# Attention by key blocks: eight score matmuls in one stretch, then the values of four heads, with the row maxima 20 turns ahead

## The chip, the cores and the metric

The kernel runs on one core of a Trainium2 chip. Its engines are TensorE (PE; its weight loads are listed as PEld), VectorE (DVE), ScalarE (ACT), GpSimd (POOL) and SyncE (SP, which only issues DMAs here). The metric is device time in microseconds, the median of several runs.

## The reference, cut to what matters

Four layers follow each other on a tensor of 8 x 1024 x 256: a recurrent mixer, a feed-forward layer, a self-attention layer and the feed-forward layer again. Only the attention layer is touched by the change:

```python
qkv = (x @ Wqkv + bqkv).reshape(B, L, 3, 16, 16)          # B = 8, L = 1024, 16 heads of 16
q, k, v = qkv[:, :, 0], qkv[:, :, 1], qkv[:, :, 2]
scores = einsum('bqhd,bkhd->bhqk', q, k) / sqrt(16)
scores = scores + slopes[None, :, None, None] * -abs(pos[None, :] - pos[:, None])
probs = softmax(scores, axis=-1)
out = einsum('bhqk,bkhd->bqhd', probs, v).reshape(B, L, 256)
x = x + (out @ Wout + bout)                                # x was layer-normed before Wqkv
```

## The kernel before, in words

The attention layer (`attention`, from L1383) works on groups of four heads: 8 batches x 4 groups = 32 groups, numbered `g`. For a group it computes every score twice.

The first time is for the maxima. `find_maxima` on TensorE (L1639) multiplies one query block of 128 rows with half of the keys (512), for one head: a "turn", 64 turns for a group. The result fills one PSUM bank. VectorE reduces it to a maximum for each query (L1896). Below, r0, r1, r2, r3 are four turns in a row. The second time is for the values. `attend` on TensorE (L1701) computes scores with keys on the partitions: one key block of 128 keys against half of the queries (512), for one head, already shifted by the maximum, which travels as an extra row of the operand. ScalarE applies the exponential to two heads at a time (L1814), and `weigh` (L1655) multiplies the result with the values. Below, c0 to c3 are the four column score matmuls of a key block, one for each head, and V is its values.

Scores contract over 64 rows only, so a head takes half of the array: row group `rg` 0 or 1 (`tile_position=(first, 0)`). A matmul on row group 0 and one on row group 1 can run side by side. The values have 17 columns, so four heads take four column tiles (`tile_position=(0, i * SLOT)`) over all 128 rows. A pair is two heads, one on each row group. `use = 2 * t + pair` counts the pairs of scores; 16 key block steps `t` make a group (8 key blocks for each half of the queries), 512 steps in all. The bias needs a correction inside one 512 wide half: `add_block_bias` (L1560) adds two matmuls of 64 columns for each score matmul of a block that is `here`. Half of the turns and half of the key blocks are.

PSUM has eight banks. Banks 0 to 3 hold the column scores, two banks for each `use`, so that pair 0 and pair 1 alternate (`scores[use % 2]`). Bank 4 holds the values. Banks 5, 6 and 7 are a ring, `misc`: every turn of the maxima takes the next of the three, and so does every other product of the layer (queries and keys, values of the tokens, transposes, the output projection). Who takes a bank waits first until its last user has been read. With nothing else in between, turn n waits for the reduction of turn n - 3:

```python
misc = Ring([banks[:, i, :] for i in (5, 6, 7)], (cleared, 1))
m, (used, n) = misc.take(("max", g, turn), (half_max_made, STEPS * g + turn + 1))
pe.wait_ge(used, n)
```

The order of all engines is written out by the same generators. `schedule` runs, for each group, `attend` side by side with the stacks of a later group (12 matmuls of 512 columns), the values of the tokens, the layer norm and the tails of earlier groups (`conclude`). `attend` itself advances `find_maxima` by `next(rows)`, twice for each turn: once for its matmul, once for its bias. The maxima run `LEAD` turns ahead of the scores; the first group's maxima run alone in `lead`. `follow` decides when the values of an earlier step are issued. Each engine executes its own list in order; a wait in it holds everything that is behind it.

## Time and profile before

| | |
|---|---|
| Median of 3 runs | 3313.69 us (3311.7 to 3315.78) |
| Span of the profiled execution | 3314.4 us |
| TensorE busy in it | 3139.1 us (95%) |
| VectorE busy | 2521.7 us (76%) |
| ScalarE busy | 1985.8 us (60%) |
| GpSimd busy | 780.8 us (24%) |
| Mean granted TensorE clock | 0.961 of 2.4 GHz |

The profiled execution's own time is its span, 3314.4 us; it lies inside the range of the runs shown. The first 800 us are the mixer and the first feed-forward layer's start, the attention layer's scores run from about 1163 us (maxima alone) and 1232 us (everything) to 2967 us, and the second feed-forward layer ends the span. A matmul's duration in a row reaches from its start to the end of its drain, so neighbours overlap; the distance from one start to the next is what TensorE really needs. A row that merges several instructions (x8) gives the start of the first and the time until the end of the last.

### The profile page before, as it was taken

How to read it: one execution, taken by the hardware profiler on the slowest of the kernel's cores; microseconds unless marked ns; L12 is line 12 of the kernel's file. 1: busy time of each engine (PE TensorE's matmuls, PEld its weight loads, DVE VectorE, ACT ScalarE, POOL GpSimd, SP SyncE). 2: the span in 40 equal slices, each digit the busy share in tenths (PEclk: the TensorE clock that was granted, in tenths of full speed). 3: DMA queues.
4: the chain of work that ended last, by engine and by line, in shares of the span. 5: the costliest groups of instructions: out<-in, count | busy, mean ns of one | idle time of the engine just before them, and what ended most of it. 6: DMA issues, size and time to landing. Idle time of an engine off the chain costs nothing. (4 is left out here: it accounts for less than half of the span.)

```text
span 3314.4 us, 79004 instructions
## 1 busy us (share of the span) xinstructions
PE 3139.1 (95%) x31780; PEld 1960.7 (59%) x31780; DVE 2521.7 (76%) x4848; ACT 1985.8 (60%) x2967; POOL 780.8 (24%) x916
## 2 busy tenths in 40 slices
PE   7999999995999689999999999999999999998999
PEld 3666666663888555555555555555555555546888
DVE  6777777755888478778878788788787887837887
ACT  2544555432666317776767676767676766775665
POOL 3445454532222201111110110111111101002222
PEclk8999999986999759999999999999999999998999
DMA  1000000003111422122222131222221312202111
GB/s 54 15 15 27 27 28 27 21 15 105 52 52 51 100 39 46 25 49 47 46 50 46 25 71 25 46 50 46 50 43 27 66 30 42 42 12 95 52 58 39
DMA packets 110349, 145.51 MB, mean 44 GB/s; under 512 B 21792, under 2 KB 94256, under 8 KB 109200
## 3 DMA queue, kind: packets, MB, share of 16 engines
q1 hardware_dynamic: 108776, 136.78, 17.5%
q8 instruction: 252, 4.13, 0.5%
q0 software_dynamic: 768, 2.77, 0.4%
q10 hardware_dynamic: 440, 0.90, 0.2%
q14 instruction: 113, 0.93, 0.1%
HBM read 53.79 MB, written 38.24 MB: 28 GB/s over the span
## 5 line engine op out<-in xcount | busy, mean ns | idle before, releaser
L1896 DVE TENSOR_REDUCE b_half_max<-banks 128x1 f32<-128x512 f32 x2048 | 1304.3, 685 | 290.5 <-PE banks L1560 174.9
L1814 ACT ACTIVATE b_p_t<-banks 128x1024 f32<-128x1024 f32 x1024 | 1040.3, 1026 | 372.1 <-PE banks L1560 231.2
L1639 PE MATMUL banks<-b_k_stack,b_q_stack 62*128 62x512 f32 x2048 | 835.0, 480 | 26.4 <-issue 10.4
L1701 PE MATMUL banks<-b_q_stack,b_k_stack 64*128 64x512 f32 x2048 | 832.9, 469 | 8.8 <-ACT b_p_t L1814 7.7
L1655 PE MATMUL banks<-b_p_t,b_v 128*17 128x256 f32 x8192 | 628.4, 385 | 0.2 <-ACT b_p_t L1814 0.2
L1701 PEld LDWEIGHTS banks<-b_q_stack,b_k_stack 64*128 64x128 f32 x2048 | 344.4, 185 | 373.0 <-issue 322.8
L1639 PEld LDWEIGHTS banks<-b_k_stack,b_q_stack 62*128 62x128 f32 x2048 | 342.0, 188 | 75.5 <-DVE b_half_max L1896 33.9
L1560 PE MATMUL banks<-b_unit,b_tables 64*128 64x64 bf16 x4096 | 373.1, 197 | 0.0
L1137 ACT ACTIVATE ffn_relu<-banks,ffn_scale_fc 128x512 f32<-128x512 f32 x256 | 176.2, 688 | 205.3 <-PE banks L1069 205.3
L1082 PE MATMUL banks<-ffn_proj_t,ffn_r_hi 128*128 128x256 f32 x1024 | 262.2, 289 | 2.7 <-DVE ffn_r_lo L1263 2.5
L1560 PEld LDWEIGHTS banks<-b_unit,b_tables 64*128 64x128 bf16 x4096 | 186.2, 96 | 120.7 <-issue 70.6
L1083 PE MATMUL banks<-ffn_proj_t,ffn_r_lo 128*128 128x256 f32 x1024 | 253.9, 281 | 0.0
L1655 PEld LDWEIGHTS banks<-b_p_t,b_v 128*17 128x17 f32 x8192 | 142.4, 95 | 169.1 <-ACT b_p_t L1814 59.3
L1999 POOL TENSOR_TENSOR b_qk_lo<-b_qk,b_qk_hi 128x512 fp32r<-128x512 f32 x64 | 82.0, 1281 | 582.4 <-ACT b_qk_hi L1754 414.9
L1082 PEld LDWEIGHTS banks<-ffn_proj_t,ffn_r_hi 128*128 128x128 f32 x1024 | 193.5, 189 | 17.9 <-DVE ffn_r_lo L1263 8.6
L1065 PE MATMUL banks<-ffn_x_hi,ffn_fc_t 128*128 128x512 f32 x512 | 203.0, 396 | 0.0
L1066 PE MATMUL banks<-ffn_x_lo,ffn_fc_t 128*128 128x512 f32 x512 | 202.6, 396 | 0.0
L1083 PEld LDWEIGHTS banks<-ffn_proj_t,ffn_r_lo 128*128 128x128 f32 x1024 | 193.4, 189 | 8.2
L1263 DVE TENSOR_TENSOR ffn_r_lo<-ffn_square,ffn_r_hi 128x512 fp32r<-128x512 f32 x256 | 188.9, 738 | 8.8
L1319 POOL TENSOR_TENSOR ffn_x<-ffn_x,ffn_scaled_out 128x256 f32<-128x256 f32 x128 | 113.1, 883 | 339.6 <-DVE ffn_scaled_out L1274 339.6
L1261 DVE CAST ffn_r_hi<-ffn_square 128x512 fp32r<-128x512 f32 x256 | 127.3, 497 | 74.5 <-ACT ffn_square L1141 72.7
L1141 ACT ACTIVATE ffn_square<-ffn_relu 128x512 f32<-128x512 f32 x256 | 161.9, 632 | 8.2
(247 smaller groups left out, 4937.7 us busy)
## 6 DMA issues: line engine op xcount, KB each, us to landing
ffn_x<-x SPq DMA_DIRECT2D x32, 512.0 KB, 3.8
b_q_stack<-b_qk_hi SPq DMA_DIRECT2D x252, 64.0 KB
b_k_stack<-b_qk_hi SPq DMA_DIRECT2D x252, 64.0 KB
a_x<-hidden_states SPq DMA_DIRECT2D x16, 512.0 KB, 4.1
x<-a_x SPq DMA_DIRECT2D x16, 512.0 KB, 2.9
x<-ffn_x SPq DMA_DIRECT2D x16, 512.0 KB, 2.8
b_x<-x SPq DMA_DIRECT2D x8, 1024.0 KB, 5.5
out<-ffn_x SPq DMA_DIRECT2D x16, 512.0 KB, 2.9
```

The source lines that it names most:

```text
L1065: pe.matmul(b, fc_t[:, kt, cols], x_hi[:, kt, :], start=kt == 0, stop=False)
L1066: pe.matmul(b, fc_t[:, kt, cols], x_lo[:, kt, :], start=False, stop=False)
L1082: pe.matmul(b[:, 0:DIM], r_hi[par][:, m, i * P:(i + 1) * P], proj_t[:, m, :], start=m == 0, stop=False)
L1083: last = pe.matmul(b[:, 0:DIM], r_lo[par][:, m, i * P:(i + 1) * P], proj_t[:, m, :], start=False, stop=m == HT - 1)
L1137: act.activation(relu[use % 2][:, :], high[use % 3], ACT.Relu, scale=scale_fc[:, m:m + 1]).then_inc(relu_made, 1)
L1263: dve.tensor_tensor(r_lo[par][:, m, :], square[use % 2][:, :], r_hi[par][:, m, :].bitcast(F32), ALU.subtract).then_inc(r_lo_made, 1)
L1560: last = pe.matmul(out[:, cols], tables[rows, g % GROUPS * PAIRS + pair, 1 - variant, part, :], unit[rows, :], start=False, stop=part == P ...
L1639: last = pe.matmul(m, q_stack[rows, slot, qb * P:(qb + 1) * P], k_stack[rows, slot, half * BANK:(half + 1) * BANK], start=True, stop=not h ...
L1655: last = pe.matmul(values[i * SLOT:i * SLOT + VW, cols], v[:, kb, hg * GROUP + i, :], p_t[(2 * t + i % 2) % P_BUFS][:, i // 2, cols], star ...
L1701: last = pe.matmul(out, k_stack[stack, slot, kb * P:(kb + 1) * P], q_stack[stack, slot, half * BANK:(half + 1) * BANK], start=True, stop=n ...
L1814: act.activation(p_t[use % P_BUFS][:, :, :], scores[use % 2], ACT.Exp, scale=slopes()[pair][0]).then_inc(p_made, 1)
L1896: dve.tensor_reduce(half_max[:, (pair + rg * PAIRS) * QB + qb, half:half + 1], misc.at["max", g, turn], axis=AX.X, op=ALU.max, negate=True ...
```

## The change

Only the attention layer's order changes; the numbers of matmuls, reductions and exponentials are the same. `attend` goes by whole key blocks. For each pair it issues the two column scores (c0, c1), then two turns of the maxima (r0, r1), then the bias corrections of the column scores and of the turns; then the same for the other pair (c2, c3, r2, r3). Only then `follow` issues the values: all eight value matmuls of the block before in one stretch. The bias corrections of two heads are interleaved, part by part. `LEAD` becomes 20 turns and `TURN`, at which the maxima of a group are transposed, 4. The other engines follow the same sequence.

```diff
-        LEAD, TURN = 16, 2
+        LEAD, TURN = 20, 4
+        BLOCKS = HALVES * QB
...
             def lead():
-                for _ in range(STEPS + LEAD):
-                    for _ in range(row_parts):
+                for _ in range((STEPS + LEAD) // ROWGROUPS):
+                    for _ in range(ROWGROUPS * row_parts):
                         next(rows)
                     yield
...
-                side_by_side(*([(STEPS, attend(g, rows), 1)] if g >= 0 else []),
-                             *([(STEPS + LEAD, lead(), 1)] if g == -1 else []),
+                side_by_side(*([(BLOCKS, attend(g, rows), 1)] if g >= 0 else []),
+                             *([((STEPS + LEAD) // ROWGROUPS, lead(), 1)] if g == -1 else []),
...
-            def follow(t, pair):
-                if pair == 0:
+            def values_of_both(t):
+                values_of(t, 0)
+                values_of(t, 1)
+
+            def follow(t):
+                step()
+                if (t - 1) % QB:
                     if (t - 2) % QB == 0:
-                        values_of(t - 2, 0)
-                        values_of(t - 2, 1)
-                        step()
-                    else:
-                        values_of(t - 2, 1)
-                elif (t - 1) % QB:
-                    values_of(t - 1, 0)
-                    step()
+                        values_of_both(t - 2)
+                    values_of_both(t - 1)
...
-            def add_block_bias(out, g, pair, rg, variant):
-
-                rows = slice(rg * STACK, (rg + 1) * STACK)
+            def add_block_bias(outs, g, pair, variant, ready):
+
                 for part in range(PARTS):
                     cols = slice(part * STACK, (part + 1) * STACK)
-                    last = pe.matmul(out[:, cols], tables[rows, g % GROUPS * PAIRS + pair, 1 - variant, part, :], unit[rows, :],
-                                     start=False, stop=part == PARTS - 1, tile_position=(rg * STACK, 0))
-                return last
+                    for rg, out in outs:
+                        rows = slice(rg * STACK, (rg + 1) * STACK)
+                        last = pe.matmul(out[:, cols], tables[rows, g % GROUPS * PAIRS + pair, 1 - variant, part, :], unit[rows, :],
+                                         start=False, stop=part == PARTS - 1, tile_position=(rg * STACK, 0))
+                        if part == PARTS - 1:
+                            last.then_inc(ready, 1)
...
+                outs = []
                 for g, turn, pair, qb, half, rg in row_turns():
...
                         last = pe.matmul(m, q_stack[rows, slot, qb * P:(qb + 1) * P], k_stack[rows, slot, half * BANK:(half + 1) * BANK],
                                          start=True, stop=not here, tile_position=(first, 0))
-                        if not here:
+                        if here:
+                            outs.append((rg, m[:, at:at + P]))
+                        else:
                             last.then_inc(row_scores, 1)
+                    yield
+                    if turn % ROWGROUPS == ROWGROUPS - 1:
+                        if outs:
+                            add_block_bias(outs, g, pair, int(qb >= CT), row_scores)
+                            outs = []
                         yield
-                        if here:
-                            add_block_bias(m[:, at:at + P], g, pair, rg, int(qb >= CT)).then_inc(row_scores, 1)
                         yield
...
-                for t, half, kb, pair, rg in turns(g):
-                    first, slot = place(g, pair + rg * PAIRS)
-                    stack, use = slice(first, first + STACK), 2 * t + pair
-                    out, here, at = scores[use % 2][:, rg, :], kb // CT == half, kb % CT * P
-                    if use >= 2:
-                        pe.wait_ge(p_made, use - 1)
-                    last = pe.matmul(out, k_stack[stack, slot, kb * P:(kb + 1) * P], q_stack[stack, slot, half * BANK:(half + 1) * BANK],
-                                     start=True, stop=not here, tile_position=(first, 0))
-                    if not here:
-                        last.then_inc(col_scores, 1)
-                    next(rows, None)
-                    if here:
-                        add_block_bias(out[:, at:at + P], g, pair, rg, int(kb < CT)).then_inc(col_scores, 1)
-                    next(rows, None)
-                    if rg == ROWGROUPS - 1:
-                        follow(t, pair)
+                for t, half, kb in key_blocks(g):
+                    here, at = kb // CT == half, kb % CT * P
+                    for pair in range(PAIRS):
+                        use, outs = PAIRS * t + pair, []
+                        if use >= 2:
+                            pe.wait_ge(p_made, use - 1)
+                        for rg in range(ROWGROUPS):
+                            first, slot = place(g, pair + rg * PAIRS)
+                            stack, out = slice(first, first + STACK), scores[use % 2][:, rg, :]
+                            last = pe.matmul(out, k_stack[stack, slot, kb * P:(kb + 1) * P], q_stack[stack, slot, half * BANK:(half + 1) * BANK],
+                                             start=True, stop=not here, tile_position=(first, 0))
+                            if here:
+                                outs.append((rg, out[:, at:at + P]))
+                            else:
+                                last.then_inc(col_scores, 1)
+                        for rg in range(ROWGROUPS):
+                            next(rows, None)
+                        if here:
+                            add_block_bias(outs, g, pair, int(kb < CT), col_scores)
+                        next(rows, None)
+                        next(rows, None)
+                    follow(t)
                     yield
...
             def attend(g, rows):
-                for t, half, kb, pair, rg in turns(g):
-                    if rg == ROWGROUPS - 1:
-                        use = 2 * t + pair
+                for t, half, kb in key_blocks(g):
+                    for pair in range(PAIRS):
+                        use = PAIRS * t + pair
                         act.wait_ge(col_scores, ROWGROUPS * (use + 1))
                         if use >= P_BUFS:
                             act.wait_ge(weighed, 2 * (t - 2))
                         if use == 0:
                             act.wait_ge(weights_split, 3)
                         act.activation(p_t[use % P_BUFS][:, :, :], scores[use % 2], ACT.Exp, scale=slopes()[pair][0]).then_inc(p_made, 1)
-                    next(rows, None)
-                    if rg == ROWGROUPS - 1:
-                        follow(t, pair)
+                        for rg in range(ROWGROUPS):
+                            next(rows, None)
+                    follow(t)
                     yield
...
             def attend(g, rows):
-                for t, half, kb, pair, rg in turns(g):
-                    next(rows, None)
-                    if rg == ROWGROUPS - 1:
-                        follow(t, pair)
+                for t, half, kb in key_blocks(g):
+                    for _ in range(GROUP):
+                        next(rows, None)
+                    follow(t)
                     yield
```

For the rows below: L1701 (before) and L1708 (after) are column scores, L1639 and L1638 turns of the maxima, L1560 and L1557 bias corrections, L1655 and L1659 values. On TensorE, a step of a key block without bias on the column scores stood like this before, in the middle of a group:

```order
L1701 MATMUL banks<-b_q_stack,b_k_stack 128x512
L1639 MATMUL banks<-b_k_stack,b_q_stack 128x512
L1560 MATMUL banks<-b_unit,b_tables 128x64 x2
L1701 MATMUL banks<-b_q_stack,b_k_stack 128x512
L1639 MATMUL banks<-b_k_stack,b_q_stack 128x512
L1560 MATMUL banks<-b_unit,b_tables 128x64 x2
L1655 MATMUL banks<-b_p_t,b_v 17x256 x4
L1701 MATMUL banks<-b_q_stack,b_k_stack 128x512
L1639 MATMUL banks<-b_k_stack,b_q_stack 128x512
L1701 MATMUL banks<-b_q_stack,b_k_stack 128x512
L1639 MATMUL banks<-b_k_stack,b_q_stack 128x512
L1655 MATMUL banks<-b_p_t,b_v 17x256 x4
```

And such a step stands like this now, on TensorE:

```order
L1708 MATMUL banks<-b_q_stack,b_k_stack 128x512 x2
L1638 MATMUL banks<-b_k_stack,b_q_stack 128x512 x2
L1557 MATMUL banks<-b_unit,b_tables 128x64 x4
L1708 MATMUL banks<-b_q_stack,b_k_stack 128x512 x2
L1638 MATMUL banks<-b_k_stack,b_q_stack 128x512 x2
L1659 MATMUL banks<-b_p_t,b_v 17x256 x8
```

Before, four value matmuls stood between the second and the third turn and four behind the fourth; now all eight stand behind the fourth turn, and two turns follow each other directly. At the change from one half of the queries to the next, the values wait for the copy of their bank. There TensorE's list was, before (the `b_pv` row is the transposes of `conclude`):

```order
L1701 MATMUL banks<-b_q_stack,b_k_stack 128x512
L1639 MATMUL banks<-b_k_stack,b_q_stack 128x512
L1560 MATMUL banks<-b_unit,b_tables 128x64 x2
L1701 MATMUL banks<-b_q_stack,b_k_stack 128x512
L1639 MATMUL banks<-b_k_stack,b_q_stack 128x512
L1560 MATMUL banks<-b_unit,b_tables 128x64 x2
L1701 MATMUL banks<-b_q_stack,b_k_stack 128x512
L1639 MATMUL banks<-b_k_stack,b_q_stack 128x512
L1701 MATMUL banks<-b_q_stack,b_k_stack 128x512
L1639 MATMUL banks<-b_k_stack,b_q_stack 128x512
L1655 MATMUL banks<-b_p_t,b_v 17x256 x8
L1667 MATMUL banks<-b_ident,b_pv 128x128 x4
```

And it is now:

```order
L1671 MATMUL banks<-b_ident,b_pv 128x128 x4
L1708 MATMUL banks<-b_q_stack,b_k_stack 128x512 x2
L1638 MATMUL banks<-b_k_stack,b_q_stack 128x512 x2
L1557 MATMUL banks<-b_unit,b_tables 128x64 x4
L1708 MATMUL banks<-b_q_stack,b_k_stack 128x512 x2
L1638 MATMUL banks<-b_k_stack,b_q_stack 128x512 x2
L1557 MATMUL banks<-b_unit,b_tables 128x64 x8
L1659 MATMUL banks<-b_p_t,b_v 17x256 x16
```

Before, one half step went without values and the next issued eight; now a whole step goes without them and the next issues sixteen.

## Rows read from the trace of the kernel before

**Rows 1.** Page: span, busy time and share of each engine

```profile
span 3314.4 us, 79004 instructions
...
PE 3139.1 (95%) x31780; PEld 1960.7 (59%) x31780; DVE 2521.7 (76%) x4848; ACT 1985.8 (60%) x2967; POOL 780.8 (24%) x916
```

**Rows 2.** Costliest groups: busy, mean ns of one | idle before, its releaser

```profile
L1896 DVE TENSOR_REDUCE b_half_max<-banks 128x1 f32<-128x512 f32 x2048 | 1304.3, 685 | 290.5 <-PE banks L1560 174.9
L1814 ACT ACTIVATE b_p_t<-banks 128x1024 f32<-128x1024 f32 x1024 | 1040.3, 1026 | 372.1 <-PE banks L1560 231.2
...
L1655 PE MATMUL banks<-b_p_t,b_v 128*17 128x256 f32 x8192 | 628.4, 385 | 0.2 <-ACT b_p_t L1814 0.2
```

**Rows 3.** Line L1701 alone: durations ns min/median/max, first and last start

```profile
L1701 PE MATMUL banks<-b_q_stack,b_k_stack x2048: 386/491/792, 1232.2 to 2966.7; 64*128 64x512 f32 x187
```

**Rows 4.** Stretches of 50 us: busy time of each engine, PEclk, DMA share, GB/s

```profile
1200.00:1250.00 50.00, 48.98 (x257) 28.57 (x256) 36.48 (x61) 12.28 (x17) 2.00 (x3) 0.63 0.11 19
...
1850.00:1900.00 50.00, 48.94 (x510) 26.54 (x509) 38.01 (x61) 35.16 (x42) 7.44 (x10) 1.00 0.23 39
```

**Rows 5.** Timeline of TensorE: start us, us, engine, line, [idle before <-releaser]

```profile
1499.91 0.49 PE L1701 MATMUL banks<-b_q_stack,b_k_stack 64*128 64x512 f32 x1
...
1500.80 0.63 PE L1655 MATMUL banks<-b_p_t,b_v 128*17 128x256 f32 x8
1501.36 0.50 PE L1701 MATMUL banks<-b_q_stack,b_k_stack 64*128 64x512 f32 x1
...
1502.18 0.63 PE L1655 MATMUL banks<-b_p_t,b_v 128*17 128x256 f32 x8
1502.73 0.50 PE L1701 MATMUL banks<-b_q_stack,b_k_stack 64*128 64x512 f32 x1
...
1855.74 0.49 PE L1701 MATMUL banks<-b_q_stack,b_k_stack 64*128 64x512 f32 x1
...
1856.07 0.40 PE L1701 MATMUL banks<-b_q_stack,b_k_stack 64*128 64x512 f32 x1
...
1856.40 0.63 PE L1655 MATMUL banks<-b_p_t,b_v 128*17 128x256 f32 x8
...
1856.96 0.49 PE L1701 MATMUL banks<-b_q_stack,b_k_stack 64*128 64x512 f32 x1
```

**Rows 6.** Timeline of VectorE: with the maxima alone, and in the middle

```profile
1213.10 5.47 DVE L1896 TENSOR_REDUCE b_half_max<-banks 128x1 f32<-128x512 f32 x9 [1.65 <-PE banks L1560]
...
1500.56 2.63 DVE L1896 TENSOR_REDUCE b_half_max<-banks 128x1 f32<-128x512 f32 x4 [0.19 <-PE banks L1560]
```

**Rows 7.** Timeline of VectorE and of TensorE, 1545 to 1548 us

```profile
1546.07 0.69 DVE L1863 TENSOR_TENSOR b_x_lo<-banks,b_x_hi 128x512 fp32r<-128x512 f32 x1 [0.69 <-ACT b_x_hi L1729]
1546.67 1.28 DVE L1896 TENSOR_REDUCE b_half_max<-banks 128x1 f32<-128x512 f32 x2
...
1545.33 0.73 PE L1639 MATMUL banks<-b_k_stack,b_q_stack 62*128 62x512 f32 x2
...
1546.90 0.46 PE L1639 MATMUL banks<-b_k_stack,b_q_stack 62*128 62x512 f32 x1
...
1547.50 0.47 PE L1639 MATMUL banks<-b_k_stack,b_q_stack 62*128 62x512 f32 x1
```

**Rows 8.** Timeline: a turn and its reduction, and a step without values

```profile
1838.95 0.50 PE L1639 MATMUL banks<-b_k_stack,b_q_stack 62*128 62x512 f32 x1
...
1839.50 0.69 DVE L1896 TENSOR_REDUCE b_half_max<-banks 128x1 f32<-128x512 f32 x1 [1.41 <-PE banks L1639]
...
1840.01 0.50 PE L1701 MATMUL banks<-b_q_stack,b_k_stack 64*128 64x512 f32 x1
...
1841.47 0.49 PE L1701 MATMUL banks<-b_q_stack,b_k_stack 64*128 64x512 f32 x1 [0.34 <-ACT b_p_t L1814]
```

**Rows 9.** Timeline of TensorE near the end of the maxima

```profile
2916.99 0.49 PE L1639 MATMUL banks<-b_k_stack,b_q_stack 62*128 62x512 f32 x1
2917.41 1.06 PE L1655 MATMUL banks<-b_p_t,b_v 128*17 128x256 f32 x16
2918.40 0.66 PE L1667 MATMUL banks<-b_ident,b_pv 128*128 128x128 f32 x4
```

More of the change, by code:

```diff
@@ L1483, in row_turns, with key_blocks @@
                 yield g, turn, pair, qb, half, 1 - turn % 2
-        def turns(g):
+        def key_blocks(g):
             for half in range(HALVES):
                 for kb in range(QB):
-                    for pair in range(PAIRS):
-                        for rg in range(ROWGROUPS):
-                            yield (g * HALVES + half) * QB + kb, half, kb, pair, rg
+                    yield (g * HALVES + half) * QB + kb, half, kb
         def tails(weigh, conclude):
@@ L1508, in step @@
                     waiting.pop(0)
-            def follow(t, pair):
-                if pair == 0:
-                    if (t - 2) % QB == 0:
-                        values_of(t - 2, 0)
-                        values_of(t - 2, 1)
-                        step()
-                    else:
-                        values_of(t - 2, 1)
-                elif (t - 1) % QB:
-                    values_of(t - 1, 0)
-                    step()
+            def values_of_both(t):
[4 more added lines that the diff above has]
+                if (t - 1) % QB:
+                    if (t - 2) % QB == 0:
+                        values_of_both(t - 2)
+                    values_of_both(t - 1)
             def finish():
-                end = ALL * HALVES * QB
-                values_of(end - 2, 1)
-                values_of(end - 1, 0)
-                values_of(end - 1, 1)
+                step()
+                values_of_both(ALL * HALVES * QB - 1)
                 while waiting:
@@ L2029, in attend @@
             def attend(g, rows):
-                for t, half, kb, pair, rg in turns(g):
-                    next(rows, None)
-                    if rg == ROWGROUPS - 1:
-                        follow(t, pair)
+                for t, half, kb in key_blocks(g):
+                    for _ in range(GROUP):
+                        next(rows, None)
+                    follow(t)
                     yield
@@ L2111, in attend @@
             def attend(g, rows):
-                for t, half, kb, pair, rg in turns(g):
-                    next(rows, None)
-                    if rg == ROWGROUPS - 1:
-                        follow(t, pair)
+                for t, half, kb in key_blocks(g):
+                    for _ in range(GROUP):
+                        next(rows, None)
+                    follow(t)
                     yield
```

## The prediction

> **What bounds the kernel now.** I read the page's busy times first [rows 1], then the costliest groups with their idle time [rows 2], then timelines of single steps. TensorE is busy for 95% of a span of 3314.4 us, VectorE for 76%, ScalarE for 60%. The reader should see in the groups that it is TensorE that the others wait for: the reductions of the maxima (2048, L1896) had 290.5 us of idle time before them, most of it ended by TensorE, the exponentials (1024, L1814) 372.1 us, while the values (L1655) had 0.2 us [rows 2]. The column scores run from 1232.2 to 2966.7 us [rows 3]: 1734.5 us for 512 key block steps, 3.39 us each.
>
> The timeline splits that. From the first column score of a half step to that of the next it is 1.45 us with bias corrections on columns and turns, 1.37 us with them on one kind, and 1.22 us with none (starts at 1499.91, 1501.36 and 1502.73, and at 1855.74 and 1856.96) [rows 5]. In a key block with column bias both halves have it and one half has a turn's bias too: 1.45 + 1.37 = 2.82 us. Without column bias it is 1.37 + 1.22 = 2.59 us. Half of the blocks are of each kind, so the mean is 2.71 us. The other 0.68 us of the 3.39 are projections, transposes and a few stalls between the steps, which change their place but not their number.
>
> VectorE is near its limit beside it. With the maxima alone nine reductions take 5.47 us [rows 6]; one takes 0.69, so they follow each other every (5.47 - 0.69)/8 = 0.60 us, and four turns cost at least 2.39 us. In the middle four took 2.63 us and then 0.19 us of waiting for TensorE [rows 6]. So TensorE sets the pace, and VectorE has 0.2 to 0.4 us a block to spare.
>
> **What the change takes away.** Eight values in one stretch cost 0.99 us, from their start to the next product (2917.41 to 2918.40) [rows 9]. Four cost 1501.36 - 1500.80 = 0.56 us [rows 5], so twice four is 1.12 us. That saves 0.13 us a block on TensorE, if it never waits: 0.13 x 512 = 67 us. I give nothing for interleaved bias corrections: they cost 0.16 us for a half step's four either way (0.82 against 0.66 us from first score to values, [rows 5]).
> The Trainium skill (TensorEngine Tiling, Key Properties) says that changing the tiling mode, not just the tile, drains the array, which speaks for this change. The trace agrees that an extra stretch costs something, the 0.13 us above.
>
> **What it adds: a loop through three banks.** This decides. Turn n may write its bank only after the reduction of turn n - 3. So the fourth turn of a block, r3, waits for the reduction of r0. Before, r0 stood at the front of the step and r3 two half steps later, with four values between them. Now r0 to r3 stand within the eight score matmuls, and all values stand behind r3. TensorE's list is in order, so what is queued behind the waiting r3 is the eight values, then the next block's c0 and c1, and then the next r0, whose reduction the next r3 waits for. That closes a loop whose every term the trace shows:
>
> 1. Start of r0's reduction to start of r3: 0.83 us. In [rows 7] the turn at 1547.50 takes the bank of the reduction that starts at 1546.67 (0.69 us of reduction, 0.14 us to TensorE; the turn at 1546.90 follows the end of the row that freed its bank, 1546.07 + 0.69 = 1546.76, by 0.14 us too).
> 2. r3 to the values: 0.42 us (2916.99 to 2917.41) [rows 9].
> 3. The eight values: 0.99 us [rows 9].
> 4. c0 and c1 to r0: 0.33 us, as the second score of a row group follows the first (1855.74 to 1856.07) [rows 5].
> 5. r0's start to the start of its reduction: 0.55 us for a turn that starts with an empty array (1838.95 to 1839.50) [rows 8]. A score behind another shows 0.40 instead of 0.49 us [rows 5], so I take 0.55 - 0.10 = 0.45.
>
> Sum: 0.83 + 0.42 + 0.99 + 0.33 + 0.45 = 3.02 us. In every block one pair of turns has bias corrections. If it is r0 and r1, they stand before the reduction of r0; if r2 and r3, before the values. Either way 0.16 us go into the loop: 3.18 us. Column bias adds another 1.45 - 1.37 = 0.08 in half of the blocks: 0.04 in the mean. The loop takes 3.22 us, against 2.71 us before.
>
> Is anything else longer? TensorE's own work is 2.71 - 0.13 = 2.58, VectorE's 2.39, ScalarE's two exponentials 2 x 1.03 = 2.05 us [rows 2]. None is, so TensorE will stand before r3 for 3.22 - 2.58 = 0.64 us in each block. Before, r0 started together with c0 and only four values stood behind r3, so the same loop was 0.83 + 0.42 + 0.56 + 0.55 = 2.36 us, with 0.16 at most for bias, where TensorE needed 2.71: slack.
>
> The projections and transposes between blocks stand between r3 and the next r0, so they come on top of the loop as they came on top of the 2.71 us, at the same cost. VectorE's other work (layer norm, reciprocals) mostly fits between r3's reduction and the next r0's, where it is idle now.
>
> The Trainium skill (TensorE: Matmul & The Clock Gate, LDWEIGHTS — get the stationary operand into the array) states that only weight loads are pulled ahead and matmuls stay in program order. That is the rule against this change: the values, whose inputs are ready, cannot pass r3. By the opposite rule the sum would be the 67 us of gain. No row of this trace shows values passing a waiting turn.
>
> **The rest.** At the start of each half of the queries TensorE had no values in one half step and waited 0.34 us for an exponential: 1840.01 to 1841.47 is 1.46 us for a half step without values, whose scores alone need 0.82 [rows 5, 8]. Such places (64) cost some 0.2 to 0.45 us more than the model above; I take 0.3, or 19 us, which go. In their place a block without values goes at VectorE's 2.39 instead of 3.22 - 0.99 = 2.23 us, 0.16 x 64 = 10 us back. The lead has 4 turns more (4 x 0.60 = 2.4 us), and there r0 becomes readable only after r1 has been let in, which leaves VectorE a gap of 0.3 to 0.5 us in 21 pairs with bias: 8 us; together 10. The end has one block less with turns, which leaves 507. The longer lead covers the later transpose of the maxima (20 - 4 = 16 turns instead of 14), so nothing for it.
>
> **Sum.** (3.22 - 2.71) x 507 = 259; - 19 + 10 + 10 = + 1. So +260 us on the profiled 3314.4 us, which is within 0.1% of the median of 3313.69: 3574 us. I state 3570.
>
> **Bounds.** Low: r0 follows c0 by only 0.23 us (the merged turns of [rows 7], 0.73 - 0.50), biases hide entirely: 3.02 - 0.10 = 2.92, or 0.21 x 507 = 106, and 20 us of stalls go: 3400. High: biases cost 0.16 more, and VectorE's other work is exposed (each batch some layer norm rows of 0.69 us as at 1546.07, [rows 7], 32 of them behind waits): 0.67 x 507 + 35 = 375, or 3690. I am nearer to the middle, since items 1, 2 and 3 (2.24 of 3.02 us) are read straight from rows.
>
> **Rivals.**
> - *The loop doesn't close, TensorE's own list decides.* For it: TensorE was never far from 49 of 50 us busy [rows 4], and the waits for banks are small now. Then 0.13 x 512 = 67 us and the stalls of 13 us are gained, 5 us lost in the lead: 3240 us, faster. It needs a loop of at most 2.58 us, 0.44 us under the 3.02 us that rows give without any bias. The point where it turns: faster below 2.71. Chance 6%.
> - *The loop is half right*, about 2.75 us, because r0 and its reduction start earlier than I have them: within 0.2% of now (that is what a measurement of this kernel can tell). 3%.
> - *The clock falls.* With waits of 0.64 us in each block the granted clock could drop as in 1200 to 1250 us (0.63, between the levels 1.2 and 2.4 GHz), where turns wait for reductions; it is 1.00 in the middle [rows 4]. At 1.2 GHz items 2 to 4 (1.74 us) would double: about +0.8 us more a block for half of the time, 3314 + 260 + 450 = about 4000 us. Against it: at 1200 TensorE streams one score for each 0.60 us, in the loop eight scores and eight values in 3.2. Chance 4%.
> - *The change doesn't do what it says:* it does; the order of the rows on TensorE is as said.
>
> **How the numbers follow.** The loop at 2.92 to 3.4 us: 87%, all slower. Clock: 4%, slower. Half right: 3% within 0.2%, rival one: 6% faster. Range for 8 in 10: 3430 to 3660, the loop from about 2.95 to 3.38 us.
>
> **What would show it.** In the profile after: idle time before L1638 with the reduction L1896 as its releaser, some 0.6 us a block, about 300 us in all; TensorE busy less than 90% in the middle; the distance from c0 to c0 3.1 to 3.3 us in blocks with nothing else; eight values in 0.99 us; VectorE busy share lower, with its reductions in a burst of four and then a gap of 0.5 us or more before r0's. Wrong would be: no wait before L1638, blocks of 2.6 us; or a PEclk below 1.00 in the middle.

## The result and the profile after

The changed kernel takes 3551.37 us (median of 4 runs, 3547.6 to 3561.75) against 3314.74 us before, measured beside it: a ratio of 1.0708 [1.0683, 1.0733], 7.1% slower. The prediction was 3570 us. The profiled execution has a span of 3545.8 us, 231.4 us more than before [rows 1].

Its page: span, then busy time and share of each engine.

```profile
span 3545.8 us, 79004 instructions
...
PE 3209.5 (91%) x31780; PEld 1954.3 (55%) x31780; DVE 2508.2 (71%) x4848; ACT 1974.4 (56%) x2967; POOL 779.6 (22%) x916
...
L1906 DVE TENSOR_REDUCE b_half_max<-banks 128x1 f32<-128x512 f32 x2048 | 1298.2, 684 | 554.9 <-PE banks L1557 364.7
L1824 ACT ACTIVATE b_p_t<-banks 128x1024 f32<-128x1024 f32 x1024 | 1017.3, 1024 | 519.3 <-PE banks L1557 338.9
...
L1659 PE MATMUL banks<-b_p_t,b_v 128*17 128x256 f32 x8192 | 549.0, 393 | 0.7 <-ACT b_p_t L1824 0.7
```

The work is the same to the instruction, and reductions and exponentials are as long as before [rows 2]. What grew is idle time: before the reductions from 290.5 to 554.9 us, before the exponentials from 372.1 to 519.3. TensorE's idle time grew from 175.3 to 336.3 us. Its busy time is 70.4 us longer for the same matmuls: a row reaches to the end of its drain, so a matmul that nothing follows at once probably counts for more, and a part ran at a lower clock (below). Every engine is less busy in share, so the cause is a wait, not work. The column scores say where:

```profile
L1708 PE MATMUL banks<-b_q_stack,b_k_stack x2048: 386/492/794, 1236.1 to 3198.1; 64*128 64x512 f32 x187
```

From the first to the last it is 1962.0 us instead of 1734.5 [rows 3]. That is 227.5 of the 231.4 us; the other 3.9 us stand before the first of them (1236.1 against 1232.2), and after the last one both kernels take 347.7 us.

The wait itself stands before the turns. The trace lists it twice: before their weight loads (PEld) and before their matmuls (PE). These are two views of the same waits, not to be added: total us, times, longest. After:

```profile
PEld banks L1638 <- DVE b_half_max L1906: 310.7, 513, 1.0
...
PE banks L1638 <- DVE b_half_max L1906: 93.7, 354, 0.7
...
PEld banks L1638 <- ACT b_qk L1766: 49.4, 62, 0.9
...
PEld banks L1638 <- ACT b_shift_full L1783: 37.3, 30, 1.2
```

And for the turns of the kernel before:

```profile
PEld banks L1639 <- DVE b_half_max L1896: 33.9, 82, 1.1
...
PEld banks L1639 <- ACT b_shift_full L1773: 14.1, 23, 0.6
...
PE banks L1639 <- DVE b_half_max L1896: 6.9, 13, 0.8
...
PEld banks L1639 <- ACT b_qk L1756: 2.5, 2, 1.3
```

In either view the reductions hold TensorE nine times as long or more. The weight load's view comes nearer to what a turn is late by: for the r3 in the next rows it is 0.67 us, the matmul's is 0.23, and r3 starts 0.63 us behind r2. In the matmul's view the end of the matmul before covers part of the wait. One round of the loop can be read from a timeline (start us, us, engine, line, and idle time before it with what ended it; each value matmul leaves two records, so eight values are a row of x16):

```profile
1632.15 0.50 PE L1708 MATMUL banks<-b_q_stack,b_k_stack 64*128 64x512 f32 x2
1632.49 0.40 PE L1638 MATMUL banks<-b_k_stack,b_q_stack 62*128 62x512 f32 x2
...
1633.00 2.48 DVE L1906 TENSOR_REDUCE b_half_max<-banks 128x1 f32<-128x512 f32 x4 [0.44 <-PE banks L1557]
1633.12 0.40 PE L1638 MATMUL banks<-b_k_stack,b_q_stack 62*128 62x512 f32 x1
1633.75 0.49 PE L1638 MATMUL banks<-b_k_stack,b_q_stack 62*128 62x512 f32 x1 [0.23 <-DVE b_half_max L1906]
1634.17 1.06 PE L1659 MATMUL banks<-b_p_t,b_v 128*17 128x256 f32 x16
1635.16 0.50 PE L1708 MATMUL banks<-b_q_stack,b_k_stack 64*128 64x512 f32 x2
1635.49 0.40 PE L1638 MATMUL banks<-b_k_stack,b_q_stack 62*128 62x512 f32 x2
...
1636.01 0.69 DVE L1906 TENSOR_REDUCE b_half_max<-banks 128x1 f32<-128x512 f32 x1 [0.52 <-PE banks L1557]
```

The reduction of r0 starts at 1633.00; r3 gets its bank at 1633.75, 0.75 us later, and had nothing else to wait for (r2 started at 1633.12). r0 and r1 share one row of 0.40 us, so they run side by side; r3 starts 0.63 us behind r2. Then 0.42 us to the values, 0.99 us to c0, 0.33 us to r0, 0.52 us to its reduction at 1636.01: 3.01 us, and from c0 to c0 the same 3.01. The four reductions form a burst, and VectorE then stands idle for 0.5 us before the next r0.

From the starts of all column scores (every fourth is a c0) comes the length of each block. Over the blocks with four turns, eight values and nothing else (202 before, 186 after) the medians are, in us:

| | no column bias | column bias | mean of all 511 |
|---|---|---|---|
| before | 2.60 | 2.83 | 3.39 |
| after | 3.01 | 3.16 | 3.84 |

### The profile page after: what moved, and what is told of

The parts are those of the page before. It is cut to its first block and busy times, and to the rows that moved or that the text cites. A ratio compares the mean times of both kernels' runs of the same rounds, so it can differ in the third digit from the quotient of the medians.

```text
span 3545.8 us, 79004 instructions
## 1 busy us (share of the span) xinstructions
PE 3209.5 (91%) x31780; PEld 1954.3 (55%) x31780; DVE 2508.2 (71%) x4848; ACT 1974.4 (56%) x2967; POOL 779.6 (22%) x916
## 3 DMA queue, kind: packets, MB, share of 16 engines
q0 software_dynamic: 768, 2.77, 0.4%
## 5 line engine op out<-in xcount | busy, mean ns | idle before, releaser
L1906 DVE TENSOR_REDUCE b_half_max<-banks 128x1 f32<-128x512 f32 x2048 | 1298.2, 684 | 554.9 <-PE banks L1557 364.7
L1824 ACT ACTIVATE b_p_t<-banks 128x1024 f32<-128x1024 f32 x1024 | 1017.3, 1024 | 519.3 <-PE banks L1557 338.9
L1638 PE MATMUL banks<-b_k_stack,b_q_stack 62*128 62x512 f32 x2048 | 703.7, 452 | 183.0 <-DVE b_half_max L1906 93.7
L1659 PE MATMUL banks<-b_p_t,b_v 128*17 128x256 f32 x8192 | 549.0, 393 | 0.7 <-ACT b_p_t L1824 0.7
L1638 PEld LDWEIGHTS banks<-b_k_stack,b_q_stack 62*128 62x128 f32 x2048 | 298.2, 191 | 455.1 <-DVE b_half_max L1906 310.7
L1708 PE MATMUL banks<-b_q_stack,b_k_stack 64*128 64x512 f32 x2048 | 520.8, 483 | 3.2 <-ACT b_p_t L1824 2.5
L1708 PEld LDWEIGHTS banks<-b_q_stack,b_k_stack 64*128 64x128 f32 x2048 | 207.0, 187 | 189.4 <-issue 154.3
L1557 PE MATMUL banks<-b_unit,b_tables 64*128 64x64 bf16 x4096 | 296.0, 197 | 0.0
L1659 PEld LDWEIGHTS banks<-b_p_t,b_v 128*17 128x17 f32 x8192 | 198.6, 99 | 175.4 <-issue 45.9
L1557 PEld LDWEIGHTS banks<-b_unit,b_tables 64*128 64x128 bf16 x4096 | 156.8, 97 | 158.9 <-issue 146.7
```

What stands on the lines that cost most here:

```text
L1557: last = pe.matmul(out[:, cols], tables[rows, g % GROUPS * PAIRS + pair, 1 - variant, part, :], unit[rows, :], start=False, stop=part == P ...
L1638: last = pe.matmul(m, q_stack[rows, slot, qb * P:(qb + 1) * P], k_stack[rows, slot, half * BANK:(half + 1) * BANK], start=True, stop=not h ...
L1659: last = pe.matmul(values[i * SLOT:i * SLOT + VW, cols], v[:, kb, hg * GROUP + i, :], p_t[(2 * t + i % 2) % P_BUFS][:, i // 2, cols], star ...
L1708: last = pe.matmul(out, k_stack[stack, slot, kb * P:(kb + 1) * P], q_stack[stack, slot, half * BANK:(half + 1) * BANK], start=True, stop=n ...
L1824: act.activation(p_t[use % P_BUFS][:, :, :], scores[use % 2], ACT.Exp, scale=slopes()[pair][0]).then_inc(p_made, 1)
L1906: dve.tensor_reduce(half_max[:, (pair + rg * PAIRS) * QB + qb, half:half + 1], misc.at["max", g, turn], axis=AX.X, op=ALU.max, negate=True ...
```

## The experiments

Ratios are to the kernel before, run beside each of them. For comparison they are turned into us on 3320 us, what the kernel before took in the first two sets (3322 and 3320 us). The changed kernel is +235 us by that.

**e1: the new order of scores and bias, the values as before.** `follow` of the kernel before is put back (the last lines of `finish` too), and every engine calls it behind each pair:

```diff
-                    follow(t)
+                        follow(t, pair)
```

> The eight score matmuls keep the new order (c0, c1, r0, r1, then c2, c3, r2, r3, bias corrections interleaved), but the values are issued as before the change, four behind each pair. Bank loop: r3 again has the other half step and four values between itself and r0, so it doesn't wait; TensorE's own list decides, a block takes 2.6 to 2.85 us and the time goes back to 3310 (3280 to 3340) us, idle time before the turns below 60 us. Rival, the new order of scores itself costs (row groups, bias corrections, later column scores for ScalarE): it stays above 3450 us.

Measured: 3314.86 us, ratio 0.9982 [0.9964, 1.0], -6 us. As the theory said for the time. The idle time was not below 60 us: before the turns' weight loads the reductions left 71.9 us (33.9 in the kernel before), before the matmuls 23.6. Timeline of e1, two half steps and the start of the third:

```profile
1644.30 5.10 DVE L1909 TENSOR_REDUCE b_half_max<-banks 128x1 f32<-128x512 f32 x8 [0.92 <-PE banks L1560]
1644.75 0.50 PE L1711 MATMUL banks<-b_q_stack,b_k_stack 64*128 64x512 f32 x2
...
1646.04 0.50 PE L1711 MATMUL banks<-b_q_stack,b_k_stack 64*128 64x512 f32 x2
...
1647.34 0.50 PE L1711 MATMUL banks<-b_q_stack,b_k_stack 64*128 64x512 f32 x2
```

Half steps of 1.29 and 1.30 us, and eight reductions in a row without a gap. With four values between r1 and r2, nothing waits here. Blocks with column bias even took 2.73 us in the median instead of 2.83, the others 2.59. The new order alone costs nothing.

**e9: the values alone.** The opposite half of the change. The kernel before, its order and its bias as they were, with all values behind r3:

```diff
             def follow(t, pair):
                 if pair == 0:
...
-                elif (t - 1) % QB:
-                    values_of(t - 1, 0)
-                    step()
+                    return
+                step()
+                if (t - 1) % QB:
+                    if (t - 2) % QB == 0:
+                        values_of_both(t - 2)
+                    values_of_both(t - 1)
```

> The kernel before, with its order of scores and turns (c0 r0 c1 r1 c2 r2 c3 r3, each turn's bias correction right behind it) and its lead of 16 turns, and only the values put together: all eight behind r3. Theory, the loop through the three banks with r0 at its earliest: start of r0's reduction to r3 0.75 us, r3 to the values 0.42, values 0.99, r0 to its reduction 0.55, in all 2.71; one bias correction in it 0.08; the like order without bias took 2.80 us instead of 2.71, so 2.88 a block without and 2.92 with column bias, 2.90 against 2.71 before, x 507 = 95 us, and some 35 us of the blocks with other work: 3440 us (3400 to 3470), ratio 1.037, steps of 2.8 to 2.9 us. Rival 1, the values in one stretch alone cost what the whole change costs, wherever r0 stands: 3550 us. Rival 2, the order of the scores made the loop long and the values in one stretch cost nothing: 3310 us or less.

Measured: 3410.71 us, ratio 1.0277 [1.0253, 1.03], +92 us, steps of 2.78 and 2.81 us. Inside the theory's range, at its lower part. Its timeline, one step:

```profile
1598.78 0.73 PE L1638 MATMUL banks<-b_k_stack,b_q_stack 62*128 62x512 f32 x2
...
1599.39 2.48 DVE L1895 TENSOR_REDUCE b_half_max<-banks 128x1 f32<-128x512 f32 x4 [0.44 <-PE banks L1559]
...
1600.14 0.49 PE L1638 MATMUL banks<-b_k_stack,b_q_stack 62*128 62x512 f32 x1
1600.56 1.06 PE L1654 MATMUL banks<-b_p_t,b_v 128*17 128x256 f32 x16
1601.55 0.50 PE L1700 MATMUL banks<-b_q_stack,b_k_stack 64*128 64x512 f32 x1
```

The same loop, 0.61 + 0.75 + 0.42 + 0.99 = 2.77 us: r0 stands beside c0, so the 0.33 us of c0 and c1 are not in it. With e1, the changed kernel and the kernel before it makes a table of two by two. The new order alone gives -6 us, the values in one stretch alone +92, both together +235: 149 us come only from the two together. In the loop that the values have closed, the reduction of r0 starts 0.85 us after c0 in the changed kernel (0.33 + 0.52) and 0.61 us after it in e9, and the steps are 0.23 and 0.35 us longer than e9's.

**e2: a shorter reduction.** It reads every second column:

```diff
-                             half:half + 1], misc.at["max", g, turn],
+                             half:half + 1], misc.at["max", g, turn][:, 0:BANK:2],
```

> The changed kernel, but each reduction of the maxima reads every second column of its bank, 256 instead of 512 (so the shift of the scores is not the full maximum). Bank loop: the reduction's 0.69 us shrinks by about 0.27 us, a quarter of a block's wait less for each block, 0.27 x 507 = 137 us: 3415 us (3390 to 3450), and the block goes from 3.02 to about 2.75 us. Rival, TensorE waits for ScalarE's exponentials or is slow by its clock: less than 30 us gained, 3520 to 3550 us.

Measured: 3358.47 us, ratio 1.0115 [1.0083, 1.0147], +38 us, 197 us less than the changed kernel. The group of the reductions in e2:

```profile
L1906 DVE TENSOR_REDUCE b_half_max<-banks 128x1 f32<-128x256 f32 x2048 | 759.2, 419 | 851.3 <-PE banks L1557 556.0
```

They sat idle for 851.3 us, so it isn't VectorE's busy time that counts, but that r3 waits for one reduction's length. Steps fell by 0.26 us in both kinds (2.75 and 2.90), 132 us in 507 blocks, close to what was expected. The other 65 us lie in blocks with other work, which the expectation had left alone; the clock is in them too, for its mean over the 34 stretches of 50 us looked at below is 0.992 instead of 0.978, at most 0.014 x 1700 = 24 us. The theory's sign and its 0.3 us a block held, its total was too small.

**e4: r3 behind the values.** On each engine `follow` stands before the last turn of the block. On TensorE the edit also takes the interleaving of the turns' bias corrections back, one turn at a time, so two things differ from the changed kernel:

```diff
-                    for _ in range(GROUP):
+                    for _ in range(GROUP - 1):
                         next(rows, None)
                     follow(t)
+                    next(rows, None)
```

> The changed kernel, but the fourth turn of a block (r3) stands behind the eight values instead of ahead of them (bias corrections follow each turn directly). Bank loop: the reduction of r0 is over long before r3 comes, so nothing waits; TensorE's list with one turn alone in the array takes 2.65 to 2.85 us a block, 3320 us (3280 to 3370). Rival, the eight values in a stretch or the order of scores are slow by themselves: above 3450 us.

Measured: 3440.38 us, ratio 1.037 [1.0334, 1.0407], +123 us. A miss by 120 us. Timeline of e4:

```profile
1575.46 0.50 PE L1638 MATMUL banks<-b_k_stack,b_q_stack 62*128 62x512 f32 x1
...
1576.00 2.48 DVE L1903 TENSOR_REDUCE b_half_max<-banks 128x1 f32<-128x512 f32 x4 [0.29 <-PE banks L1638]
...
1576.74 0.50 PE L1638 MATMUL banks<-b_k_stack,b_q_stack 62*128 62x512 f32 x1
...
1577.25 1.06 PE L1654 MATMUL banks<-b_p_t,b_v 128*17 128x256 f32 x16
1578.24 0.50 PE L1638 MATMUL banks<-b_k_stack,b_q_stack 62*128 62x512 f32 x1
```

The loop didn't go, it moved on by one turn. r3, now behind the values (1575.46), is reduced from 1576.00; the next block's r2, three turns later, waits for that and starts at 1576.74; behind r2 stand the values, and behind them r3 again: 0.54 + 0.74 + 0.51 + 0.99 = 2.78 us. The medians over e4's steps are 2.70 and 2.77. I had asked which turn waits across the values in the old place, and not which one does in the new place. Wherever all eight values stand, between turn k and turn k + 1, turn k waits for the reduction of turn k - 3, which is the turn behind the last values.

**e5: turns beside columns, values together.** c0 r0 c1 r1 c2 r2 c3 r3:

```diff
                                 last.then_inc(col_scores, 1)
-                        for rg in range(ROWGROUPS):
                             next(rows, None)
```

> The changed kernel, all eight values in one stretch, but the turns stand beside the column scores again (c0, r0, c1, r1, c2, r2, c3, r3). Bank loop, with the terms as the changed kernel's trace has them: r0's reduction to r3 0.75, r3 to the values 0.43, values 0.99, r0 beside c0 and 0.55 to its reduction, about 0.1 of bias corrections: 2.8 to 2.85 us a block instead of 3.0 to 3.16, so 507 x 0.25 = 127 us less than the changed kernel, 3425 us (3390 to 3460). It stays slower than the kernel before, whose stretches of values are half as long. Rival, the order of scores plays no part and only the length of the stretch of values does: 3550 us. Rival, the stretch of values costs nothing if turns stand beside columns: 3310 us.

Measured: 3555.93 us, ratio 1.0691 [1.0656, 1.0726], +229 us. A miss by 130 us: as slow as the changed kernel. The timeline of e5, a step where r0 and r1 have bias, and below it one where r2 and r3 have it:

```profile
1632.25 0.73 PE L1638 MATMUL banks<-b_k_stack,b_q_stack 62*128 62x512 f32 x2
...
1632.83 0.23 PE L1557 MATMUL banks<-b_unit,b_tables 64*128 64x64 bf16 x4
...
1633.10 2.48 DVE L1905 TENSOR_REDUCE b_half_max<-banks 128x1 f32<-128x512 f32 x4 [0.67 <-PE banks L1557]
...
1664.62 0.49 PE L1638 MATMUL banks<-b_k_stack,b_q_stack 62*128 62x512 f32 x1
...
1665.15 1.29 DVE L1905 TENSOR_REDUCE b_half_max<-banks 128x1 f32<-128x512 f32 x2 [0.30 <-PE banks L1638]
```

Without bias on r0 its reduction starts 0.53 us after it, and that block takes 2.84 us (1664.61 to 1667.45). With bias it starts 0.85 us after it, since the corrections of both turns stand behind r1. In the changed kernel that is 0.33 us for c0 and c1 and 0.52 us, again 0.85. So the interleaved corrections take away what moving r0 forward gives, in the blocks where r0 has them: there the medians are 3.06 us without and 3.18 with column bias. Where r2 and r3 have them it is 2.81 and 2.84, where the changed kernel has 3.01 and 3.07. e9 has each correction right behind its turn, reaches 0.61 us and has 2.77 to 2.81 us in all four kinds. By these medians the corrections account for 0.29 and 0.37 us in half of the blocks, some 85 of the 137 us between e5 and e9; e9 differs from e5 in the lead too, which e6 shows to cost nothing. But e5 should also have ended below the changed kernel by the 0.2 us of the other half of the blocks, about 50 us, and is level with it. A part is the clock: 20 of the 34 stretches below 1.00 and a mean of 0.970, against 16 and 0.978, at most 14 us more. What takes the rest wasn't found.

**e3, e8, e10, e7: the values two blocks behind.** The lag is always two, so no block goes without values and none has those of two blocks:

```diff
                 step()
-                if (t - 1) % QB:
-                    if (t - 2) % QB == 0:
-                        values_of_both(t - 2)
-                    values_of_both(t - 1)
+                values_of_both(t - 2)
```

e3 is that on the changed kernel, e8 on e5, e10 on e9, and e7 on e1 (with `values_of(t - 2, pair)`).

> The changed kernel, but the values always follow two key blocks behind their scores, so that each block issues eight values: no block without values and none with sixteen. Bank loop alone: blocks in the middle keep 3.02 and 3.16 us. The 64 places where a block without values is followed by one with sixteen cost 0.8 us and a short spell at half clock now: 50 us less, 3500 us (3480 to 3520). Rival, these places cost nothing beyond the loop: 3550 us.

Measured: 3505.63 us, ratio 1.0561 [1.0533, 1.0588], +186 us, 49 less than the changed kernel. As expected; the steps stay at 3.01 and 3.16 us. The gain sits in the two blocks of each half that the lag changes: the second took 2.87 us and now 3.40, the third 5.22 and now 3.92, 0.77 x 64 = 49 us.

> Turns beside the column scores and all values in one stretch, two key blocks late, so no block without values and none with sixteen. Theory: the loop of 2.8 to 2.85 us stays, the 64 places that cost the changed kernel 45 us (3551 to 3506) go as well: 45 us below the same kernel without the lag, 3380 us (3345 to 3410). Rival, the two effects are one: no difference between these two.

Measured: 3496.0 us, ratio 1.0515 [1.0484, 1.0546], +171 us. A miss by 116 us: the lag gave 58 us, but most of e5's miss is carried over.

> As e9, and the values follow two key blocks behind in every step, so that no step goes without values and none with sixteen. Theory: the gain of this lag adds to the rest as it did twice (46 us from the changed kernel, 60 us from the one with turns beside columns): 3385 us (3350 to 3420), ratio 1.02, no stretch in the middle with a granted clock below 1.00. Rival: with the loop shorter the gain is smaller, and the waits for the copy of the value bank eat it, as with the values split in fours (26 us more): 3440 to 3465 us.

Measured: 3404.68 us, ratio 1.0255 [1.0228, 1.0282], +85 us. Here the lag gave 7 us, and the intervals of e9 and e10 overlap. The time is near the upper end of the theory's range, but a gain like e3's was not there. The rival is half right: the gain is smaller, but its time, 3440 us or more, is missed too. The sign that the theory gave, no stretch in the middle below 1.00, did not come either: 9 of the 34 were, in a profiled execution that was 24 us slower than the median.

> The kernel of the split values (four behind each pair), but each half step issues its four values two key blocks late, so no half step is without values and none has eight. Theory: blocks stay at 2.6 to 2.8 us and the 64 places where TensorE waited 0.2 to 0.5 us for an exponential go, but at 64 places the values now wait for the copy of their bank, 0.3 us: 3300 us (3290 to 3320). Rival, that copy costs more than the doubling did: 3330 us or more.

Measured: 3340.57 us, ratio 1.0068 [1.0042, 1.0094], +23 us, 29 more than e1. The rival's time was right. What TensorE waited for in e7, with the transposes of `conclude` (L1668), total us, times, longest:

```profile
PE banks L1668 <- ACT b_pv L1788: 12.6, 31, 0.8
PE banks L1668 <- ACT b_shift_full L1780: 8.7, 7, 1.2
```

Before, the first of these waits was 0.8 us in all. With the values of a half ending a block later, the transposes come right behind the copy of their bank. That copy is 12.6 of the 29 us; how the rest divides wasn't separated. So the lag of two helps only where blocks without values hurt.

**e6: a lead of 16.**

```diff
-        LEAD, TURN = 20, 4
+        LEAD, TURN = 16, 4
```

> The changed kernel with LEAD = 16 turns instead of 20, TURN stays 4. Bank loop: the lead does not matter to it; four turns less at the start and one block more with turns at the end, the transposed maxima arrive in time: 3550 us, within 6 us of the changed kernel. Rival, the longer lead is part of the loss: 3530 us or less; rival, 12 turns are too few for the transposes and their way through memory: above 3570 us.

Measured: 3557.12 us, ratio 1.07 [1.0666, 1.0733]. Nothing, as expected.

## Why the prediction was right, and what in it was off

**The cause was right.** The wait stands before r3, for r0's reduction, once a block; TensorE's busy share in the middle fell from 98% to 90% (means of 34 stretches of 50 us; 12 of them lie below 90%, so that sign was met only at the edge); the distance c0 to c0 was 3.01 to 3.16 us where 3.1 to 3.3 was said; eight values took 0.99 us; VectorE works in bursts; r3 starts 0.63 us behind r2, where 0.64 us of waiting was said, and the weight loads of the turns waited 310.7 us for reductions, where about 300 us was said. Undoing the values removes all of it (e1), shortening the reduction shortens the step by as much (e2), and with r0 at the front the same loop is shorter (e9). That holds for the step; why e5, with r0 at the front too, ends no earlier than the changed kernel is only in part explained. The Trainium skill (TensorE: Matmul & The Clock Gate, LDWEIGHTS — get the stationary operand into the array) keeps matmuls in program order. The trace agrees: the values had their inputs (before L1659 the matmuls waited 0.7 us for exponentials in all, their weight loads 3.0 us), and still started 0.42 us behind the waiting r3.

**The sizes of the loop's terms.** By the timelines above, r0's reduction to r3 took 0.75 us, not 0.83: in [rows 7] the turn starts 0.14 us after the reduction, here 0.06 us (1633.00 + 0.69 to 1633.75). Bias was 0.16 us in the sum. It is 0.07 where r0 has it: 0.52 us to the reduction, where the term of the sum was 0.45. Where r3 has it, this step of the changed kernel shows it:

```profile
1638.51 0.40 PE L1638 MATMUL banks<-b_k_stack,b_q_stack 62*128 62x512 f32 x2
...
1638.95 2.63 DVE L1906 TENSOR_REDUCE b_half_max<-banks 128x1 f32<-128x512 f32 x4 [0.46 <-PE banks L1638]
...
1639.69 0.50 PE L1638 MATMUL banks<-b_k_stack,b_q_stack 62*128 62x512 f32 x1 [0.31 <-DVE b_half_max L1906]
...
1640.20 1.06 PE L1659 MATMUL banks<-b_p_t,b_v 128*17 128x256 f32 x16
```

Here r0's reduction starts after 0.44 us, as the sum had it, and r3 to the values is 0.51 us, 0.09 more than the 0.42 of [rows 9]. Column bias cost 0.15 us where it stands, a mean of 0.08 instead of 0.04. Together the loop is 3.01 and 3.16, a mean of 3.09 instead of 3.22. Against 2.71 before, which was right (2.60 and 2.83), that is 0.37 x 507 = 188 us, not 259. The step that was mis-sized is this one, by 71 us. It is a sum of medians; blocks of the same kinds with a stall in them took longer in both kernels.

**What made up for it.** That 3570 us came within 19 us of the measured time is in part luck: 71 us too many in the loop, and some 40 too few beside it. The score stage became 227.5 us longer, so 40 us have another place, and the prediction had only 1 us there: "projections and transposes ... at the same cost" was wrong. Two things stand in it.

First, waits for other users of the three banks. The turns' weight loads waited 49.4 us for ACT's reading of the new queries and keys (b_qk), 2.5 before. ACT reads such a bank twice, 778 and 769 ns in its groups. The third turn behind it wants the bank, and in the new order it comes sooner, with no four values before it. e1, with values between, has 8.0 us of that wait; e9 35.2, e4 47.2.

Second, the clock. PEclk 1.00 was said for the middle. Of the 34 stretches of 50 us from 1250 to 2950 us, 16 are below 1.00 in the changed kernel, none before. These are stretches of it (us, busy time of PE, PEld, DVE, ACT, POOL, PEclk, DMA share, GB/s):

```profile
1800.00:1850.00 50.00, 45.49 (x414) 22.35 (x406) 36.92 (x73) 29.30 (x34) 7.92 (x11) 0.93 0.22 38
1850.00:1900.00 50.00, 44.77 (x468) 22.31 (x466) 37.17 (x60) 32.80 (x37) 4.36 (x6) 1.00 0.17 30
1558.00:1560.00 2.00, 2.00 (x19) 1.03 (x22) 1.50 (x3) 1.46 (x2) 1.32 (x3) 0.50 0.01 4
1560.00:1562.00 2.00, 2.00 (x32) 0.73 (x21) 0.80 (x2) 0.49 (x1) 0.00 (x0) 0.67 0.04 8
```

At 1558 TensorE runs at 1.2 GHz. It is the block behind the one without values, and its stretch of sixteen value matmuls stands in these rows of the changed kernel:

```profile
1559.43 2.82 PE L1659 MATMUL banks<-b_p_t,b_v 128*17 128x256 f32 x32
1562.18 0.50 PE L1708 MATMUL banks<-b_q_stack,b_k_stack 64*128 64x512 f32 x2
```

It takes 2.75 us to the next product. 50 of the 64 such stretches take 1.85 us, at a granted clock of 1.00; the other 14, wholly or partly at 1.2 GHz, take 2.71 to 3.54, together 18 us more than at 1.85 each. The mean granted clock over the 34 stretches is 0.978, so at most 0.022 x 1700 = 37 us are lost. In e3 the blocks without values are gone, and here is the first of these stretches in it:

```profile
1800.00:1850.00 50.00, 44.29 (x451) 21.57 (x451) 37.48 (x63) 30.77 (x35) 5.24 (x9) 1.00 0.22 39
```

6 of 34 are below 1.00, their mean is 0.995, and 49 us are gained; at most 0.017 x 1700 = 29 of them are the clock. e8 gained 58 us with a mean clock that rose from 0.970 to 0.984, at most 24 us. So the clock is a part and not the whole of what the blocks without values cost. How the 40 us divide between clock, bank waits and the half changes stays open.

**The rest.** For the half changes (64) I had -19 + 10 us. By their place in the half, the blocks without values and the ones behind them took 2.87 + 5.22 us in the mean, before 3.22 + 4.47: 0.40 more, where two steady blocks became 0.74 longer. That is 22 us better in 64 places instead of 9. But the first block of a half grew by 1.14 us, since other work changed its place, so these means don't separate the half changes from the rest. The lead's 10 us were 3.9 at the start. By the prediction the values had 0.2 us of idle time before them. That is the row of their matmuls; their weight loads waited 59.3 us for exponentials before the change and 3.0 after it, of which the prediction has no word. What that is worth in time isn't shown.

**The rivals.** That TensorE's own list decides (6%) is refuted by e1 and e2, the loop of 2.75 us (3%) by the steps of 3.01 and 3.16; the clock rival (4%) had the right mechanism in a few short stretches, at a twelfth of its price or less. The 0.13 us that a stretch of eight values saves is real (0.99 against 1.12 us), but no kernel here could cash it: each one with eight in a stretch has steps of 2.70 us or more.

**A version that beats both.** None was found. e1 is the best, within 0.2% of the kernel before. The loop says why eight values in a stretch don't pay with three banks: at its shortest it is 0.75 + 0.42 + 0.99 + 0.54 = 2.70 us without any bias, from the rows of e9 and e4, against a mean of 2.71 us before.

## What to carry to other kernels

When the users of a ring of n banks share an in-order engine with other work, add up the loop: turn k waits for the reader of turn k - n, and everything that stands between is in it. Gathering small pieces into one long stretch saves each piece's switch, but puts the whole stretch into one gap between two turns, and the ring must bridge it. Moving the stretch past one turn only hands the wait to the next. And two edits can cost more together than their sum (-6 and +92 us apart, +235 together): measure them as two by two.

## What the runs showed of the hardware

- The granted clock fell to 1.2 GHz for a few us at a time in the middle of a stage that is 90% busy (0.50 in 1558 to 1560 us), after a block of waits and without values; before the change no stretch of 50 us there was below 1.00. e1 and e9, whose TensorE is busy for 97 and 96% of the time there, had 5 of 34 below 1.00, so the waits of the loop aren't the only thing that goes with it.
- A reduction of 128 x 256 with every second column took 419 ns against 684 ns for 512 columns in a row.
- Four bias corrections of 64 columns, two for each of two turns, added 0.07 to 0.09 us to the loop, not the 0.16 us that starts before had suggested.
- A turn that waited for its bank started 0.06 us after the end of the reduction that freed it (1633.69 to 1633.75).
